# Second logits stage: TensorE transposes normalised rows one chunk later, VectorE inverts the softmax sums inside the chunk

## The reference

```python
x = L0_attn_x
x = x + 0.5 * _L0_ffn_ref(_layernorm(x), ...)   # mixture of experts, 8 experts, top 2
x = x + _L0_attn_ref(_layernorm(x), ...)        # causal attention, 16 heads of 16
x = x + 0.5 * _L0_ffn_ref(_layernorm(x), ...)   # the same experts again
```

## Time and profile before

| | us |
|---|---|
| median of 3 runs | 1246.88 (1240.87 to 1252.59) |
| the profiled execution, its own time | 1247.35 |
| its span, first to last instruction | 1245.6 |
| outside the span | 1.75 |
| the second logits stage in it: first attention rows landed, to the last logits | 913.5 to 978.45 |

### The profile page before, as it was taken

One profiled execution on the slowest core, in us unless ns is written; L12 is line 12 of the kernel. 1 busy time (PEld: TensorE's weight loads), 2 busy tenths in 40 slices (PEclk: granted clock), 3 DMA queues, 4 the chain that ended last, 5 costly groups with the idle time before them and its releaser, 6 DMA issues. The chain is left out here.

```text
span 1245.6 us, 22513 instructions
## 1 busy us (share of the span) xinstructions
PE 1054.3 (85%) x6981; PEld 638.5 (51%) x6988; DVE 829.1 (67%) x2536; ACT 665.9 (53%) x1668; POOL 384.4 (31%) x404
## 2 busy tenths in 40 slices
PE   3539999993997999999999999999869369999950
PEld 2327888881442344444444444444347248888850
DVE  6774444435978888888888888888037754444428
ACT  5604455542772566666666666667636315545520
POOL 5506777762002000000000000000048226777740
PEclk9558999996997799999999999999979659999985
DMA  8502333325865344444444444440057113333329
GB/s 297 197 4 90 102 103 103 104 88 215 219 233 123 53 62 61 62 62 61 62 62 62 61 62 62 62 61 11 10 192 249 51 39 94 103 107 103 102 103 361
DMA packets 90816, 132.53 MB, mean 106 GB/s; under 512 B 29968, under 2 KB 59088, under 8 KB 90704
## 3 DMA queue, kind: packets, MB, share of 16 engines
q1 hardware_dynamic: 72848, 89.65, 31.1%
q0 software_dynamic: 13632, 37.24, 9.4%
q10 hardware_dynamic: 4224, 4.19, 1.0%
HBM read 82.42 MB, written 48.23 MB: 105 GB/s over the span
## 5 line engine op out<-in xcount | busy, mean ns | idle before, releaser
L1415 ACT ACTIVATE stacks_rows_or_prob<-stacks_bank 128x512 f32<-128x512 f32 (+3 forms) x768 | 326.0, 495 | 142.8 <-PE stacks_bank L1347 117.6
L1429 DVE CUSTOM_DVE_ANT_0 stacks_bank<-stacks_bank,all_causal 128x128 f32<-128x128 f32 (+3 forms) x512 | 245.3, 504 | 32.6 <-PE stacks_bank L1318 28.9
L1432 DVE TENSOR_REDUCE t_maxp<-stacks_bank 128x1 f32<-128x512 f32 x256 | 175.5, 685 | 25.0 <-PE stacks_bank L1318 24.5
L1358 PE MATMUL stacks_bank<-stacks_rows_or_prob,stacks_turned_or_values 128*32 128x512 f32 (+3 forms) x1536 | 164.5, 500 | 3.0 <-ACT stacks_rows_or_prob L1415 1.1
L1318 PE MATMUL stacks_bank<-stacks_kst,stacks_qst 96*128 96x512 bf16 (+2 forms) x528 | 159.8, 347 | 7.9 <-DVE t_maxp L1429 4.4
L1344 PE MATMUL stacks_bank<-stacks_qst,stacks_kst 99*128 99x512 bf16 (+3 forms) x528 | 154.5, 333 | 2.7 <-ACT stacks_rows_or_prob L1415 1.9
L1296 POOL COPY stacks_turned_or_values<-stacks_values 128x512 f32<-128x512 f32 x16 | 9.8, 613 | 426.8 <-DMA stacks_kst<-qk_parts 285.9
L1318 PEld LDWEIGHTS stacks_bank<-stacks_kst,stacks_qst 96*128 96x128 bf16 x528 | 48.4, 98 | 125.6 <-DVE t_maxp L1429 66.7
L653 PE MATMUL ae_psG<-a_w,ae_xT 128*128 x426 | 112.7, 401 | 0.0
L653 PE MATMUL be_psG<-b_w,be_xT 128*128 x426 | 112.2, 399 | 0.0
L1347 PE MATMUL stacks_bank<-all_causal_t,all_ident_bf 128*128 128x128 bf16 x512 | 109.5, 221 | 0.0
(11 more groups left out here) (294 smaller groups left out, 1897.6 us busy)
## 6 DMA issues: line engine op xcount, KB each, us to landing
stacks_qst<-qk_parts SPq DMA_DIRECT2D x66, 128.0 KB, 5.0
stacks_kst<-qk_parts SPq DMA_DIRECT2D x66, 128.0 KB, 7.6
stacks_rows_or_prob<-y_rows SPq DMA_DIRECT2D x16, 512.0 KB, 5.9
s_yk<-y_rows SPq DMA_DIRECT2D x16, 512.0 KB, 7.6
stacks_parts_or_stacks<-qk_parts SPq DMA_DIRECT2D x60, 128.0 KB, 6.2
qk_parts<-stacks_parts_or_stacks SPq DMA_DIRECT2D x16, 384.0 KB, 2.7
qk_parts<-q_parts SPq DMA_DIRECT2D x16, 384.0 KB, 3.6
o_rows<-t_orow SPq DMA_DIRECT2D x32, 136.0 KB, 9.0
```

Of the source, the lines that this page charges most:

```text
L1358: ins = nc.tensor.matmul(psO[c][h * VW:(h + 1) * VW, a - c * 512:512], vst[k][:, j, h * VW:(h + 1) * VW], prob[j % 2][:, h, a:(c + 1) * 51 ...
L1415: nc.scalar.activation(prob[j % 2][:, h, a:(c + 1) * 512], psS[n % ST_BANKS][:, a - c * 512:512], ACT.Exp, scale=DK ** -0.5).then_inc(exp_ ...
L1429: ins = nc.vector.tensor_tensor_reduce(psR[bank][:, 0:w], psR[bank][:, 0:w], T.causal[:, 512 - w:512], 1.0, -BIG, ALU.add, ALU.max, maxp[: ...
L1432: ins = nc.vector.tensor_reduce(maxp[:, h, col:col + 1], psR[bank][:, 0:w], AX_X, ALU.max)
```

## The change

`TURN` and `SCORE` are 2 and 3 in the second logits stage (1 and 2 in the first, as they were). PE transposes `xn` of chunk c - 2 instead of c - 1 in step c, and works out logits of chunk c - 3 instead of c - 2; ACT's copies follow. `steps` runs one step longer in this stage (in the first it ends where it did). On DVE the inversion of chunk c + 2 moves from the head of the step to the place between block 1 and block 2.

```diff
@@ steps
-            for c in range(-2, CH + 2):
+            for c in range(-2, CH + SCORE):
@@ VectorE
-            def step(c, b, has):
+            def invert(c, b, has):
                 if has(2):
                     dve.wait_ge(raw_loaded[b], (c // 2) * 16 + 32)
                     wait(dve, att_ready, c * U + U)
                     nc.vector.reciprocal(inv[:, b], raw[:, b, :, :, DK]).then_inc(inv_ready, 1)
+
+            def step(c, b, has):
                 if not has(0):
+                    invert(c, b, has)
                     return
                 for s in range(U):
+                    if s == 2:
+                        invert(c, b, has)
@@ TensorE
-                    if has(-2) and s == 0:
-                        scores(c - 2)
+                    if has(-SCORE) and s == 0:
+                        scores(c - SCORE)
                     if attended and has(1):
                         turn_att(c + 1, 1 - b, s)
-                    if has(-1):
-                        turn(c - 1, 1 - b, s)
-                    if has(-2) and s == 2:
-                        turn_scores(c - 2)
+                    if has(-TURN):
+                        turn(c - TURN, (c - TURN) % 2, s)
+                    if has(-SCORE) and s == 2:
+                        turn_scores(c - SCORE)
@@ ScalarE
-                    if has(-1):
-                        copy_turned(c - 1, s)
+                    if has(-TURN):
+                        copy_turned(c - TURN, s)
...
```

More of the change, by code:

```diff
@@ L169, in phase_logits @@
         BY_DVE = U if attended else U // 2
+        TURN = 2 if attended else 1
+        SCORE = TURN + 1
         def normalised_rows(eng, n):
@@ L373, in step @@
                 for s in range(U):
-                    if has(-2) and s == 1:
-                        act.wait_ge(l_done, c * 2 - 3)
+                    if has(-SCORE) and s == 1:
+                        act.wait_ge(l_done, (c - SCORE) * 2 + 1)
                         nc.scalar.copy(lT[:], psL[0][:, 0:P]).then_inc(l_copied, 1)
@@ L381, in step @@
                         nc.scalar.copy(aT[:, s], psA[s % 2][:, 0:D].rearrange("p (k t) -> p k t", k=DC)).then_inc(aT_ready, 1)
-                    if has(-1):
-                        copy_turned(c - 1, s)
+                    if has(-TURN):
+                        copy_turned(c - TURN, s)
                     if has(0) and s == 1 and not attended:
                         normalise(c, b)
-                    if has(-2) and s == 3:
-                        act.wait_ge(l_done, c * 2 - 2)
-                        nc.scalar.copy(logits[:, bass.ds((c - 2) * U, U), :],
+                    if has(-SCORE) and s == 3:
+                        act.wait_ge(l_done, (c - SCORE) * 2 + 2)
+                        nc.scalar.copy(logits[:, bass.ds((c - SCORE) * U, U), :],
                                        psL[1][:, 0:P].rearrange("p (s e) -> p s e", s=U)[:, :, 0:E]).then_inc(l_copied, 1)
```

## The result

The change makes the kernel slower by 0.8%: the median went from 1246.88 us to 1259.42 us (13 executions each, 1240.87 to 1262.58 before and 1250.58 to 1270.65 after), a ratio of 1.0082 with a 95% interval of 1.0054 to 1.0110. The ratio leaves out executions over 1.5% above the fastest of their kernel (one on either side); the two medians, over all, lie 1.0% apart. The forecast was 1247.8 with a range that ended at 1253.5, so the measured median lies 5.9 us above the range.

A forecast was written before the change was run, and what follows sets the result against it. A ring of waits between VectorE and TensorE, not one engine, bound the kernel at 6.90 us a chunk. With -2.9 ahead of the last chunk and +3.86 at the end, about +0.9 on 1246.88 gave 1247.8, range 1241.5 to 1253.5.

The forecast's parts named there:

- The two rings: Loops of waits between VectorE and TensorE: the first sets the 6.90 us period, the second 6.67; with the change 6.44.
- Step 1: Inversion leaves the head of the step, -0.46 us a chunk, hidden in VectorE's 0.63 wait for the third projection.
- Step 2: GpSimd's `bl_att` gets its inverses about 1 us later; 2.0 us of slack are left, so this costs nothing.
- The price of the overlap: GpSimd's `bl_att` would lie 0.70 us over VectorE's normalising instead of 0.24; the trace gave it no price.
- The skill against the sum: Passage weighing that overlap against the skill's shared-port rule, by which up to one `bl_att` instruction blocks VectorE each chunk.
- normalising takes over 1.5: Sign that the forecast is wrong: four normalised rows of a chunk on VectorE take over 1.5 us (1.38 before).
- The port rival: VectorE and GpSimd share a port: one `bl_att` of 0.59 us blocks in each of 5 chunks, +3.0, 1250.8; chance 0.07.
- The clock rival: TensorE's clock falls waiting for chunk 1's first add: 5.1 us longer, 1252.9, chance 0.05; three chunks or more, 0.01.
- Step 5: End of the stage: chunk 6's copies and logits, then chunk 7's, add 3.86 us (2.84 with the clock up).

The follow-up runs named there:

- small split, with the change: The changed kernel with GpSimd's weight split in this stage cut to 16 of 768 columns: 1246.32 us, ratio 1.0000 against the kernel before.

## Why the prediction was wrong, point by point

Split into pieces at the starts of the normalising groups, the three timelines of VectorE read so:

| piece, us | before | small split, with the change | after |
|---|---|---|---|
| first inversion to rows of chunk 0 | 12.61 | 11.17 | 11.67 |
| rows of chunk 0 to 1 | 6.79 | 6.17 | 6.16 |
| 1 to 2 | 6.99 | 6.37 | 11.62 |
| 2 to 3 | 6.90 | 6.49 | 6.49 |
| 3 to 4 | 6.90 | 6.48 | 10.00 |
| 4 to 5 | 6.90 | 6.48 | 6.49 |
| 5 to 6 | 6.60 | 6.49 | 9.43 |
| 6 to 7 | 6.27 | 6.26 | 6.27 |
| rows of chunk 7 to last logits | 4.99 | 7.30 | 8.35 |

- **The two rings, right.** The forecast was 6.44 for the period, measured 6.48 without blocks. Chunks 0 to 7 together: 47.35 before, 44.74 with the small split, -2.6 where the forecast had -2.9. In the changed kernel itself the intervals without a block are these same ones, within 0.01. TensorE's wait for `bl_xn` is gone in the steady part, as said.
- **Step 1, the cover of the inversion, right in the steady part, and at the start only in part.** It fits into VectorE's wait as said. In its new place it starts at 927.12 under a split (926.01 to 929.64) and takes 0.54. Its last clause, that the inversion of step 0 frees nothing, holds in the profile that it was read from (no wait of TensorE there before) and not in general: in the nine kernels that have it behind the first statistics the first piece takes 11.17 to 12.42, and in the four that have it at the head 12.61 to 13.31. In three of these four (not in the kernel before) TensorE waits 0.69 to 1.62 for an add behind the inversion, which waits for its load. The piece also depends on when TensorE's clock rises: the second projection of chunk 0 takes 1.91 before and 1.30 after. The two kernels with the inversion moved and 1.91 there took 12.42 and 12.40, so most of the -0.94 of after can be the clock; how much is open.
- **Step 2, what the inversion feeds, right, and not where the loss came from.** `bl_att` isn't late for TensorE (one wait of 0.3 from 928 to 962 us), and where rows were blocked GpSimd had not waited for the inverses either.
- **The price of the overlap, under "The skill against the sum": the step that failed.** That `bl_att` would lie 0.70 over the rows instead of 0.24 was forecast, and it came so (949.09 to 949.74, 0.65). But the overlap was priced at nothing, since 0.24 of it had cost nothing: I took one safe overlap for the price of overlapping. The runs show some 0.4 for the rows under `bl_att`, and 1.5 to 1.6 for each row that it pushes behind a split's start, +7.35 in three chunks. The sign "normalising takes over 1.5" was on record and came. The rows of before held a first price: in chunk 1 the overlap was 0.36 and the row took 0.51 instead of 0.41, in the timelines of VectorE and GpSimd (before):

```profile
932.90 0.51 DVE L839 TENSOR_SCALAR bl_xn<-all_x,bl_moments,bl_rstd 128x256 f32<-128x256 f32 x1
932.64 0.62 POOL L231 TENSOR_TENSOR bl_att<-bl_raw,bl_inv 128x256 f32<-128x256 f32 x1
```

- **The port rival, right in its mechanism and far too small in its size.** It had one `bl_att` of 0.59 in five chunks, +3.0, and a chance of 0.07. The block of about 0.4 by `bl_att` does occur. But it is only the trigger; most of the price is the rows that then take 1.9 to 2.0 instead of 0.4 under a split instruction: 4 of them, and 7.35 with the blocks by `bl_att` in the same groups. The split was in the earlier trace rows, 0.22 behind the start of the last row, and I never asked what happens if a row comes later than that. The Trainium skill, "SBUF — State Buffer", section "SBUF: two separate sides", states the rule in full: the pair is held for a whole instruction. On the length of a block this case's trace agrees (0.82, 2.03 and 3.53 us with instructions of about 0.7, 1.86 and 3.45), but for some 0.25 at the end of GpSimd's record (last section).
- **A blocked chunk is followed by a free one.** The block delays the adds and the next rows by more than GpSimd, whose next `bl_att` is over before them: it ends at 939.81 and 956.34, and the rows start at 942.60 and 959.09. So three chunks were hit and not six.
- **The clock rival, wrong in place and in size.** At 926.68, where I had put it, TensorE waits 1.96 and the clock stays at 1.00. It falls behind the waits of 4.17, 2.10 and 2.10 that the blocks make. Against the small split the intervals with a block are 5.25 + 3.52 + 2.94 = 11.71 longer; 7.35 of it are the blocks. The other 4.36 (1.68, 1.63 and 1.05) goes with TensorE at its lower level: from the start of the third projection to the last add it takes 4.12, 4.17 and 3.62 in the three chunks, against 2.55 in chunk 3 with the clock up, and that is 4.26 of it. I had 5.1 for one chunk.
- **Step 5, the end, near.** From the first copy behind the last conversion (982.30) to the end of the last logits it takes 7.33, forecast 7.8 with the lower clock and 6.8 with the upper, before 3.97. These are ScalarE's rows, then TensorE's `scores` of chunk 6, 1.00 long, and of chunk 7, 0.64 long, at the upper level. Two of over 1 us had been forecast; the piece from the rows of chunk 7 on grew by 3.36 where the forecast took 3.86:

```profile
982.30 0.36 ACT L365 COPY bl_xT<-bl_psT 128x256 f32<-128x256 f32 x1
...
989.45 0.18 ACT L395 COPY all_logits<-bl_psL 128x32 f32<-128x32 f32 x1 [0.42 <-PE bl_psL L343]
```
```profile
984.12 1.00 PE L337 MATMUL bl_psL<-bl_xT,all_gateT 128*32 128x128 f32 x16 [0.46 <-ACT bl_xT L365]
...
988.06 0.64 PE L337 MATMUL bl_psL<-bl_xT,all_gateT 128*32 128x128 f32 x16 [0.46 <-ACT bl_xT L365]
```

The sum of after by pieces: -0.94 ahead of chunk 0, then -2.6 for the rings, +7.35 for the blocks, +4.36 for the clock, and +3.36 for the end: 11.5, as measured.

What was wrong with the chances: by the ratio the result is within the 1% that was given 0.98, so that chance held; it was the range that failed. It was built without a long GpSimd instruction in any case, although the page of the Trainium skill named a mechanism whose unit in this kernel is 1.86 (one of the split's two instructions, 3.64 together), in a row that was on the table. The upper bound of an overlap's cost should have been the longest GpSimd instruction near it, once per chunk: with 1.86 in five chunks the rival would have read +9.3, and the range would have gone up to 1257 at least.

## What to carry to other kernels

Where VectorE runs an instruction of the kind that was held here (fp32 `tensor_scalar`, SBUF to SBUF) beside GpSimd, price an overlap by the length of the GpSimd instruction that can be hit, not by whether the overlap there is now costs anything: margins of 0.12 to 0.22 us stood between no cost and 1.5 to 1.6 per row. A shorter period shifts the engines against each other, so work out the new distances too. Before instructions are moved on VectorE, look at what starts on GpSimd just behind them, and read the maximum of a tile's instruction beside its median. If such an overlap can't be avoided, cut GpSimd's long instruction into short ones: six pieces instead of two took the loss from 0.8% to nothing that can be measured, without touching the order. The second stage is still 2.80 longer than before then, and a part of the total was won in the first stage; the kernel before with six pieces was not run.

## What the hardware did that I had not expected

- VectorE's normalising instruction (fp32, SBUF to SBUF) is held by a GpSimd instruction, but the inversion (0.54 under a split at 948.09, 0.55 at 913.50 with GpSimd idle), the adds with an operand in PSUM and the statistics (0.42 each, as elsewhere) are not. In the timeline after, all of these ran under the split from 926.01 to 929.64:

```profile
927.12 0.54 DVE L253 RECIPROCAL bl_inv<-bl_raw 128x64 f32<-128x64 f32 x1
927.82 0.42 DVE L264 TENSOR_TENSOR all_x<-all_x,bl_psW 128x256 f32<-128x256 f32 x1 [0.16 <-PE bl_psW L312]
928.15 0.42 DVE L822 BATCH_NORM_STATS2 bl_stats<-all_x 128x6 f32<-128x256 f32 x1
...
926.01 3.63 POOL L144 TENSOR_TENSOR b_w<-b_w 128x768 fp32r<-128x768 f32 x2 [2.16 <-ACT b_w L138]
```

- By the records the boundary isn't exact. A row that starts 0.12 ahead of a split isn't held (before, chunk 1: 933.98, split 934.10, whose first instruction then took 1.97 instead of 1.86), one 0.08 ahead is (after, chunk 1: 932.09, split 932.17). And the release comes ahead of the end of GpSimd's record: the held row of 950.47 ends at 952.36, and with its own 0.40 it must have begun at 951.96, 0.25 ahead of the record's end at 952.21. That would explain why 0.24 of overlap with `bl_att` was free before, and why 0.36 cost 0.10.
- Added work of 0.37 us per chunk cost 15.7 us in eight chunks, five times its own length.
- The first logits stage has held rows in both kernels: the longest normalising instruction there is 1972 ns before and 1974 after, against a median of 406. Seven rows take 1.97 there, each starting 0.01 to 0.02 ahead of a GpSimd instruction of 1.80 to 1.81. It was in the kernel all along, and a look at that tile before the forecast would have given the price.
